# GpSimd computes the quantization factors, and the attention scores are made with the context stationary in two column tiles

## The chip, the core and the metric

The kernel runs on one core of a Trainium2 chip. The number told is the device time in microseconds of one execution, the median of several. A core has TensorE (matmul), VectorE, ScalarE and GpSimd, and SyncE issues the DMAs; each engine takes its own instructions in order, and they wait for each other through semaphores. In the profile these are PE (its weight loads PEld), DVE, ACT, POOL and SP.

## The reference

x is 8 batches of 512 tokens of 512 numbers, ctx_2048 is 8 contexts of 64 rows of 512, of which some are masked. An attention of the layer-normed tokens over the 64 context rows is added to x, and then a feed-forward part with ternary weights and inputs quantized per token; D is 512 and the hidden width H is 2048. Cut to what matters (LN and xattn stand for the written-out functions):

```python
def _linear_bit(x, w, g):
    xq = _act_quant(_rmsnorm(x, g))        # round(x * 127/max|x|) per row
    wq = _ternary_quant(w)                 # -1, 0, 1 times arctanh(mean|w|)
    return jnp.einsum('bsd,od->bso', xq, wq)

x = x + xattn(_layernorm(x), ctx_2048, mask)     # softmax(x ctx^T / sqrt(D)) ctx
h = silu(_linear_bit(LN(x), w1, g1)) * _linear_bit(LN(x), w2, g2)
x = x + _linear_bit(h, w3, g3)
```

_rmsnorm is g * x / sqrt(mean(x*x) + 1e-8), and _act_quant clips the row's maximum from below at 1e-4.

## The kernel before

The tokens are taken in 32 tiles of 128, four to a batch; X holds all of them in SBUF. The matmuls of the feed-forward part run in float16 on integers: the quantized inputs are numbers up to 127 times 2^-24, whose rounding is the quantization, and W1q, W2q, W3q hold the ternary weights. The work on a tile t is this:

- The a-stage makes the two quantized inputs of the up projections. GpSimd makes anm, the negated mean (stage_a_mean); ScalarE squares the centred tile (stage_a_var); VectorE multiplies the centred tile by the two gains into ga (stage_a_gain) and reduces it to the two maxima am (stage_a_max); GpSimd makes ak, the reciprocal root, with a power (stage_a_root). Then the factors (stage_a_factor, on VectorE): aa is am times ak with the floor, ar its reciprocal, af is ar times ak times 127. GpSimd multiplies ga by af into c12 (quantize_12), makes asc and asq from aa (stage_a_worth), and SyncE transposes c12 by DMA into q12T.
- up(t, n) for n = 0 to 3, on TensorE: 4 matmuls with W1q into the PSUM bank S1[n % 2] and 4 with W2q into S2[n % 2]. ScalarE makes silu from S1 (line 693), VectorE multiplies it by S2 into hp (gate, line 907), GpSimd multiplies by the gain g3 into gh (gain_3, line 521), VectorE takes the maximum of gh (max_3, line 913), and ScalarE squares hp in two halves (line 700).
- The h-stage makes the factor of the third quantization: GpSimd adds the two sums of squares into hs and makes hve and hk, a reciprocal root (stage_h_root); VectorE reduces the four maxima to hm1 (stage_h_top) and makes hkk, ha, the reciprocal hr and hf (stage_h_factor). ScalarE scales gh by hf into c3 (quantize_3, line 685), SyncE transposes c3 into q3T.
- down(t) on TensorE: 16 matmuls into DN (line 1191). VectorE makes hsc, the worth of the result (worth_3), and adds DN times hsc to x (result, line 947).

There is one ga, one c12, one am, ar, af and ak. So stage_a_gain of tile t + 2 waits until quantize_12 of tile t + 1 is done, and stage_a_gain waits for anm of its own tile.

The order is written out by hand: a batch is four slots j = 0 to 3, and slot j is one call of slot(b, j) in the program of each engine. In slot t = 4b + j TensorE runs up(t, 0), down(t - 2), up(t, 1), up(t, 2), up(t, 3). Batch 0, batches 6 and 7 are written out, and batches 1 to 5 are one hardware loop. The a-stage runs one to two tiles ahead of the up projections.

The attention of batch b + 1 runs within batch b: in slot 0 TensorE turns the centred context (attention_ccT) and makes the scores, VectorE the softmax's differences; in slot 1 ScalarE makes the exponentials, TensorE turns them and makes half of the readout, VectorE adds it to x (attention_x1, line 865); the other half follows in slots 2 and 3. attention_scores runs 16 float32 matmuls of 64 columns: the stationary operand is a block of 128 tokens of x, turned beforehand in HBM (xTs), and the moving one is ccT; the result lies with tokens on partitions in R[1], where VectorE reads it. attention on GpSimd makes the scale of the exponent (xve, xrs, rs) in slot 0.

## Time and profile before

| | |
|---|---|
| median of 3 runs | 471.03 us (470.67 to 472.04) |
| profiled execution | 472.33 us |
| its span, first to last instruction | 470.5 us |
| mean granted TensorE clock, share of full speed | 0.942 |
| TensorE busy | 409.9 us (87%) |
| VectorE busy | 407.1 us (87%) |
| ScalarE busy | 339.5 us (72%) |
| GpSimd busy | 341.3 us (73%) |

Busy time is the union of an engine's instructions, without its waits. The shares are means over a prologue (weights are loaded, summed and made ternary), the steady batches, and a last batch without attention; what one stage is bound by is read from that stage's rows. In a row of the timeline the first number is the start, the second how long the instruction or the merged group lasted, and the bracket at the end the idle time before it and what ended it. Neighbouring instructions overlap by some 0.03 to 0.17 us, so costs in a row of work are best taken from start to start.

### The profile page before, as it was taken

What the parts mean: (1) busy time and instruction counts of PE and PEld (TensorE: products, weight loads), DVE (VectorE), ACT (ScalarE), POOL (GpSimd) and SP (SyncE); (2) the same over time, 40 slices, a digit from 0 to 9 for tenths busy, and PEclk for the clock granted to TensorE, in tenths of its full rate; (3) what the DMA queues carried; (4) which work ended last, traced back from release to release, by engine and by line L of the source; (5) the groups of instructions that cost most, each with busy time, mean ns of one, the idle gap of its engine ahead of it and who ended that gap; (6) DMA issues with size and microseconds to landing.
All of it is one profiled execution on the core that took longest, in us unless ns stands there. A gap on an engine that the chain in (4) does not pass through costs nothing. (4 is left out here: it accounts for less than half of the span.)

```text
span 470.5 us, 8445 instructions
## 1 busy us (share of the span) xinstructions
PE 409.9 (87%) x1966; PEld 197.5 (42%) x1966; DVE 407.1 (87%) x927; ACT 339.5 (72%) x607; POOL 341.3 (73%) x539
## 2 busy tenths in 40 slices
PE   8326644899999999999999999999999999999995
PEld 8102412344644464446434543445444634334432
DVE  3799576889899999999999999999999999999662
ACT  1585446986798769886988788878886796666552
POOL 0267858787777787788788787778777877878650
PEclk9756795899999999999999999999999999999998
DMA  7999901545557455745574466447654444444431
GB/s 270 396 366 421 312 16 22 135 90 114 139 148 173 90 114 143 179 88 115 165 178 89 111 182 163 90 111 189 139 129 111 91 88 91 86 94 91 90 69 45
DMA packets 110504, 67.45 MB, mean 143 GB/s; under 512 B 100752, under 2 KB 100880, under 8 KB 106768
## 3 DMA queue, kind: packets, MB, share of 16 engines
q1 hardware_dynamic: 110480, 67.19, 53.9%
q8 instruction: 8, 0.13, 0.1%
q14 instruction: 16, 0.13, 0.1%
HBM read 34.14 MB, written 8.39 MB: 90 GB/s over the span
## 5 line engine op out<-in xcount | busy, mean ns | idle before, releaser
L521 POOL TENSOR_TENSOR stageB<-stageB,g3b 128x512 f32<-128x512 f32 x128 | 163.8, 1285 | 46.2 <-DVE stageB L907 45.3
L1163 PE MATMUL S<-W2q,q12T 128*128 128x512 f16 x512 | 134.5, 386 | 8.9 <-DVE stageB L907 6.2
L1163 PE MATMUL S<-W1q,q12T 128*128 128x512 f16 x512 | 135.3, 388 | 0.0
L693 ACT ACTIVATE sg<-S,asc 128x512 f32<-128x512 f32 x128 | 87.5, 683 | 54.1 <-PE S L1163 49.3
L1191 PE MATMUL DN<-W3q,stageB 128*128 128x512 f16 x512 | 118.7, 386 | 7.3 <-DMA stageB<-stageB 7.3
L907 DVE TENSOR_TENSOR stageB<-sg,S 128x512 f32<-128x512 f32 x128 | 86.7, 677 | 19.9 <-ACT sg L693 10.5
L913 DVE TENSOR_REDUCE hm<-stageB 128x1 f32<-128x512 f32 x128 | 86.5, 677 | 0.2 <-POOL stageB L521 0.2
L1163 PEld LDWEIGHTS S<-W2q,q12T 128*128 128x128 f16 x512 | 49.5, 99 | 75.3 <-DVE stageB L907 13.9
L1191 PEld LDWEIGHTS DN<-W3q,stageB 128*128 128x128 f16 x512 | 49.8, 99 | 70.3 <-issue 10.8
L1163 PEld LDWEIGHTS S<-W1q,q12T 128*128 128x128 f16 x512 | 49.8, 100 | 66.3 <-issue 10.1
L685 ACT ACTIVATE stageB<-stageB,hf 128x1024 f16<-128x1024 f32 x64 | 69.8, 1140 | 4.8 <-DVE hf L933 4.8
L700 ACT ACTIVATE junk<-stageB 128x1024 bf16<-128x1024 f32 x64 | 67.3, 1051 | 6.5 <-DVE stageB L907 5.9
L874 DVE SCALAR_TENSOR_TENSOR ga<-X,anm,g12b 128x512 f32<-128x512 f32 x64 | 56.8, 925 | 5.5 <-POOL c L510 3.8
L675 ACT ACTIVATE junk_a<-X,anm 128x512 bf16 (+1 forms) x32 | 23.0, 718 | 33.2 <-POOL anm L464 33.2
L510 POOL TENSOR_SCALAR c<-ga,af 128x512 f16<-128x512 f32 x64 | 43.5, 692 | 1.1 <-DVE af L898 1.0
L880 DVE TENSOR_REDUCE am<-ga 128x2 f32<-128x1024 f32 x32 | 38.7, 1209 | 0.0
L947 DVE SCALAR_TENSOR_TENSOR X<-DN,hsc,X 128x512 f32 (+1 forms) x32 | 24.0, 750 | 10.0 <-PE DN L1191 4.5
L1123 PEld LDWEIGHTS R<-ccT,xTs 128*128 128x128 f32 x256 | 30.0, 193 | 1.8 <-ACT ccT L632 0.6
L1123 PE MATMUL R<-ccT,xTs 128*128 128x64 f32 x256 | 29.6, 274 | 0.5 <-ACT ccT L632 0.5
L475 POOL TENSOR_TENSOR ak<-avk,mhalf 128x1 f32<-128x1 f32 x32 | 27.3, 853 | 2.7
L1151 PE MATMUL DN<-wabs,ones 128*128 128x5 f32 (+1 forms) x6 | 1.8, 365 | 26.6 <-DVE wabs L953 18.2
L865 DVE SCALAR_TENSOR_TENSOR X<-R,rval,X 128x512 f32 (+1 forms) x32 | 22.6, 744 | 1.8 <-PE R L1142 1.8
(112 smaller groups left out, 430.7 us busy)
## 6 DMA issues: line engine op xcount, KB each, us to landing
xTs<-in_xT SPq DMA_DIRECT2D x8, 1024.0 KB, 7.0
X<-in_x SPq DMA_DIRECT2D x8, 1024.0 KB, 6.0
out_x<-X SPq DMA_DIRECT2D x32, 256.0 KB, 2.9
X<-in_w1T SPq DMA_DIRECT2D x4, 1024.0 KB, 12.5
stageB<-in_w2T SPq DMA_DIRECT2D x4, 1024.0 KB, 20.4
X<-in_w3T SPq DMA_DIRECT2D x4, 1024.0 KB, 9.2
ctxr<-in_ctx SPq DMA_DIRECT2D x16, 128.0 KB, 3.1
ctxc<-in_ctx SPq DMA_DIRECT2D x8, 128.0 KB, 3.9
```

Of the source, the lines that this page charges most:

```text
L510: nc.gpsimd.tensor_scalar(c12[:, i * D:(i + 1) * D], ga[:, i, :], af[:, i:i + 1], QUANTUM, ALU.mult, ALU.mult).then_inc(s_c12_made, 1)
L521: nc.gpsimd.tensor_tensor(gh[q][:, part], hp[:, part], g3b[:, part], ALU.mult).then_inc(s_gh_made, 1)
L685: nc.scalar.activation(c3[:, part], gh[q][:, part], ACT.Copy, scale=hf[:, :]).then_inc(s_c3_made, 1)
L693: nc.scalar.activation(sg[n % 2][:, :], S1[n % 2][:, :], ACT.Silu, scale=asc[z][:, 0:1])\
L700: nc.scalar.activation(junk[:, h * HALF:(h + 1) * HALF], hp[:, h * HALF:(h + 1) * HALF], ACT.Square, accum_out=hss[:, h:h + 1]).then_inc(s ...
L874: nc.vector.scalar_tensor_tensor(out=ga[:, i, :], in0=xtile(t), scalar=anm[:, :], in1=g12b[:, i, :], op0=ALU.add, op1=ALU.mult).then_inc(s ...
L880: nc.vector.tensor_reduce(am[:, :], ga[:, :, :], AX_X, ALU.max, apply_absolute_value=True)\
L907: nc.vector.tensor_tensor(hp[:, n * CH:(n + 1) * CH], sg[n % 2][:, :], S2[n % 2][:, :], ALU.mult)\
L913: nc.vector.tensor_reduce(hm[:, n:n + 1], gh[q][:, n * CH:(n + 1) * CH], AX_X, ALU.max, apply_absolute_value=True).then_inc(s_gh_max, 1)
L1123: mm = nc.tensor.matmul(R[1][:, j * M:(j + 1) * M], xTs[:, k, j, :], ccT[:, k, :], start=(k == 0), stop=(k == KD - 1))
L1163: mm = nc.tensor.matmul(bank[n % 2][:, :], q12T[q][:, i * KD + k, :], w[:, n, k, :], start=(k == 0), stop=(k == KD - 1))
L1191: mm = nc.tensor.matmul(DN[:, :], q3T[:, k, :], W3q[:, k, :], start=(k == 0), stop=(k == KH - 1))
```

## The change

It has two parts.

**Factors.** stage_a_factor, stage_h_factor and worth_3 move from VectorE to GpSimd. VectorE keeps the reciprocals, and takes them of the maxima am and hm1 themselves, right behind the reductions. The factor is then made in one instruction as a minimum: af = min(ar * 1e-4, ak), and the constant 127 * 2^-24 / 1e-4 goes into quantize_12; hkk takes the same constant, ha = max(hm1 * hkk, 127 * 2^-24), hf = min(hr * 127 * 2^-24, hkk), and hsc takes the constant out again. aa and af are made for both columns at once, in one instruction each instead of two. hsc is now double, ha single.

**Scores.** The context ccT is the stationary operand, 64 columns wide, in two column tiles (columns 0 to 63 and 64 to 127 of the array): e = 0 takes the token blocks 0 and 2, e = 1 the blocks 1 and 3, 256 moving columns each; 8 matmuls instead of 16. The result has context rows on partitions. ScalarE copies it to half (attention_half), and two transposes on TensorE (attention_turn) bring it to the layout of before in R[1]. In the loop attention_half stands behind silu 1 of slot 0, ahead of the x squares and quantize_3, and attention_turn between up(t, 2) and up(t, 3).

The diff, cut to its core:

```diff
+            def stage_a_factor(t, z):
+                pool.wait_ge(s_a_am, t + 1)
+                pool.wait_ge(s_a_k, t + 1)
...
+                nc.gpsimd.tensor_scalar(aa[z][:, :], am[:, :], ak[:, :], ACT_MAX_FLOOR, ALU.mult, ALU.max)
...
+                pool.wait_ge(s_a_r, t + 1)
+                nc.gpsimd.tensor_scalar(af[:, :], ar[:, :], ACT_MAX_FLOOR, ak[:, :], ALU.mult, ALU.min)
...
@@ quantize_12
-                    nc.gpsimd.tensor_scalar(c12[:, i * D:(i + 1) * D], ga[:, i, :], af[:, i:i + 1], QUANTUM,
+                    nc.gpsimd.tensor_scalar(c12[:, i * D:(i + 1) * D], ga[:, i, :], af[:, i:i + 1], QMAX * QUANTUM / ACT_MAX_FLOOR,
...
@@ stage_h_root, behind hk
+                pool.wait_ge(s_h_k, t + 1)
+                nc.gpsimd.tensor_scalar(hkk[:, :], hk[:, :], asc[z][:, 1:2], QMAX * QUANTUM / ACT_MAX_FLOOR, ALU.mult, ALU.mult)
+            def stage_h_factor(t):
+                pool.wait_ge(s_h_kk, t + 1)
+                pool.wait_ge(s_h_max, t + 1)
...
+                nc.gpsimd.tensor_scalar(ha[:, :], hm1[:, :], hkk[:, :], QMAX * QUANTUM, ALU.mult, ALU.max)
+                pool.wait_ge(s_h_r, t + 1)
...
+                nc.gpsimd.tensor_scalar(hf[:, :], hr[:, :], QMAX * QUANTUM, hkk[:, :], ALU.mult, ALU.min)
+            def worth_3(t, q):
...
+                nc.gpsimd.tensor_scalar(hsc[q][:, :], ha[:, :], wc[:, 2:3], ACT_MAX_FLOOR / (QMAX * QUANTUM), ALU.mult, ALU.mult)
@@ slot of GpSimd
                     stage_h_root(t - 1, (j - 1) % NZ)
+                    stage_h_factor(t - 1)
+                    if not (first and j == 1):
+                        worth_3(t - 1, (j - 1) % 2)
                 if ahead:
                     stage_a_mean(t + 2, (j + 2) % TPB)
                 if not (last and j == TPB - 1):
+                    stage_a_factor(t + 1, (j + 1) % NZ)
                     quantize_12(t + 1)
@@ slot of ScalarE
                 if attn and j == 0 and not first:
+                    attention_half(b + 1)
                     two(x_square, b + 1, 2)
@@ VectorE: stage_a_max and stage_h_top get the reciprocal, stage_a_factor, stage_h_factor and worth_3 go
+                nc.vector.reciprocal(ar[:, :], am[:, :]).then_inc(s_a_r, 1)
...
+                nc.vector.reciprocal(hr[:, :], hm1[:, :]).then_inc(s_h_r, 1)
@@ TensorE
-                for j in range(TPB):
-                    for k in range(KD):
-                        mm = nc.tensor.matmul(R[1][:, j * M:(j + 1) * M], xTs[:, k, j, :], ccT[:, k, :],
-                                              start=(k == 0), stop=(k == KD - 1))
+                for k in range(KD):
+                    for e in range(2):
+                        mm = nc.tensor.matmul(R[1][e * M:(e + 1) * M, 0:TPB // 2 * P], ccT[:, k, :], xTs[:, k, e::2, :],
+                                              start=(k == 0), stop=(k == KD - 1), tile_position=(0, e * M))
+            def attention_turn(a):
+                pe.wait_ge(s_half_made, a + 1)
+                for i in range(TPB // 2):
+                    mm = nc.tensor.transpose(R[1][:, i * P:(i + 1) * P], half[:, i * P:(i + 1) * P], identf[:, :])
```

The first place is slot 3 of batch 0 on GpSimd, a slot without attention work there, from hs of tile t - 1 (behind gain_3) to the next gain_3. Of the kernel before:

```order
L526 TENSOR_TENSOR hs<-hss 128x1
L529 TENSOR_SCALAR hve<-hs,asq 128x1
L531 TENSOR_TENSOR hk<-hve,mhalf 128x1
L464 TENSOR_SCALAR anm<-x1sum 128x1
L510 TENSOR_SCALAR c<-ga,af 128x512 x2
L482 TENSOR_TENSOR asc<-aa,wc 128x2
L485 TENSOR_SCALAR asq<-asc 128x1
L521 TENSOR_TENSOR stageB<-stageB,g3b 128x512
```

and of the changed one:

```order
L544 TENSOR_TENSOR hs<-hss 128x1
L547 TENSOR_SCALAR hve<-hs,asq 128x1
L549 TENSOR_TENSOR hk<-hve,mhalf 128x1
L552 TENSOR_SCALAR hkk<-hk,asc 128x1
L561 TENSOR_SCALAR ha<-hm,hkk 128x1
L566 TENSOR_SCALAR hf<-hr,hkk 128x1
L574 TENSOR_SCALAR hsc<-ha,wc 128x1
L467 TENSOR_SCALAR anm<-x1sum 128x1
L487 TENSOR_SCALAR aa<-am,ak 128x2
L493 TENSOR_SCALAR af<-ar,ak 128x2
L528 TENSOR_SCALAR c<-ga,af 128x512 x2
L500 TENSOR_TENSOR asc<-aa,wc 128x2
```

Six instructions are new: four between hk and anm, two between anm and the quantization c.

The second place is the same slot on VectorE, from the last reduction of hm (tile t - 1) over ga (tile t + 2) to am. Of the kernel before:

```order
L919 TENSOR_REDUCE hm<-hm 128x1
L924 TENSOR_SCALAR hkk<-hk,asc 128x1
L927 TENSOR_SCALAR ha<-hm,hkk 128x1
L929 RECIPROCAL hr<-ha 128x1
L933 TENSOR_SCALAR hf<-hr,hkk 128x1
L874 SCALAR_TENSOR_TENSOR ga<-X,anm,g12b 128x512 x2
L907 TENSOR_TENSOR stageB<-sg,S_1 128x512
L940 TENSOR_SCALAR hsc<-ha,wc 128x1
L947 SCALAR_TENSOR_TENSOR X<-DN,hsc,X 128x512
L907 TENSOR_TENSOR stageB<-sg,S_0 128x512
L880 TENSOR_REDUCE am<-ga 128x2
```

and of the changed one:

```order
L969 TENSOR_REDUCE hm<-hm 128x1
L973 RECIPROCAL hr<-hm 128x1
L934 SCALAR_TENSOR_TENSOR ga<-X,anm,g12b 128x512 x2
L955 TENSOR_TENSOR stageB<-sg,S_1 128x512
L980 SCALAR_TENSOR_TENSOR X<-DN,hsc,X 128x512
L955 TENSOR_TENSOR stageB<-sg,S_0 128x512
L942 TENSOR_REDUCE am<-ga 128x2
L947 RECIPROCAL ar<-am 128x2
```

hkk, ha, hf and hsc are gone, hr is the reciprocal of hm, and ar now stands right behind am.

The third place is slot 0 of the loop on ScalarE, from silu 1 to silu 2. Of the kernel before:

```order
L693 ACTIVATE sg<-S_1,asc 128x512
L663 ISA
L663 ACTIVATE junk_x,xss<-X,xnm 128x512
L663 ISA
L663 ACTIVATE junk_x,xss<-X,xnm 128x512
L680 REGISTER_ALU
L685 ACTIVATE stageB<-stageB,hf 128x1024 x2
L692 REGISTER_ALU
L693 ACTIVATE sg<-S_0,asc 128x512
```

and of the changed one:

```order
L750 ACTIVATE sg<-S_1,asc 128x512
L689 COPY half<-R 128x256
L720 ISA
L720 ACTIVATE junk_x,xss<-X,xnm 128x512
L720 ISA
L720 ACTIVATE junk_x,xss<-X,xnm 128x512
L737 REGISTER_ALU
L742 ACTIVATE stageB<-stageB,hf 128x1024 x2
L749 REGISTER_ALU
L750 ACTIVATE sg<-S_0,asc 128x512
```

The copy into half stands between silu 1 and the two x squares; quantize_3 and silu 2 are behind it as before.

## Rows read from the trace of the kernel before

**Rows 1.** Busy us of PE, PEld, DVE, ACT, POOL in one loop batch; clock; DMA.

```profile
212.31:261.76 49.45, 48.35 (x240) 23.09 (x239) 46.69 (x110) 40.09 (x77) 39.26 (x61) 1.00 0.57 135
```

**Rows 2.** Waits in that batch: engine, line, waited-for: us in total, times, longest.

```profile
POOL stageB L521 <- DVE stageB L907: 6.4, 9, 1.6
...
PE S L1163 <- DVE stageB L907: 1.1, 2, 0.6
POOL hs L526 <- ACT junk L700: 1.1, 2, 0.6
```

**Rows 3.** Timeline of GpSimd in slots 0 and 1 of that batch.

```profile
222.92 0.19 POOL L449 TENSOR_SCALAR xve<-xss 128x4 f32<-128x4 f32 x1
...
224.73 2.50 POOL L521 TENSOR_TENSOR stageB<-stageB,g3b 128x512 f32<-128x512 f32 x2
227.72 0.19 POOL L526 TENSOR_TENSOR hs<-hss 128x1 f32<-128x1 f32 x1 [0.49 <-ACT junk L700]
...
228.44 0.55 POOL L531 TENSOR_TENSOR hk<-hve,mhalf 128x1 f32<-128x1 f32 x1
229.07 0.19 POOL L464 TENSOR_SCALAR anm<-x1sum 128x1 f32<-128x1 f32 x1
229.24 1.36 POOL L510 TENSOR_SCALAR c<-ga,af 128x512 f16<-128x512 f32 x2
...
230.93 0.27 POOL L485 TENSOR_SCALAR asq<-asc 128x1 f32<-128x1 f32 x1 [0.17 <-POOL asc L482]
...
233.10 0.94 POOL L475 TENSOR_TENSOR ak<-avk,mhalf 128x1 f32<-128x1 f32 x1
...
240.27 0.19 POOL L526 TENSOR_TENSOR hs<-hss 128x1 f32<-128x1 f32 x1 [0.58 <-ACT junk L700]
```

**Rows 4.** Timeline of VectorE: batch 0 slot 2, then slot 1 of the batch.

```profile
94.75 1.42 DVE L874 SCALAR_TENSOR_TENSOR ga<-X,anm,g12b 128x512 f32<-128x512 f32 x2 [0.30 <-POOL c L510]
...
230.75 0.16 DVE L919 TENSOR_REDUCE hm<-hm 128x1 f32<-128x4 f32 x1
...
231.79 1.84 DVE L874 SCALAR_TENSOR_TENSOR ga<-X,anm,g12b 128x512 f32<-128x512 f32 x2
233.55 0.20 DVE L940 TENSOR_SCALAR hsc<-ha,wc 128x1 f32<-128x1 f32 x1
233.97 0.75 DVE L947 SCALAR_TENSOR_TENSOR X<-DN,hsc,X 128x512 f32 x1 [0.21 <-DVE hsc L940]
...
237.55 0.68 DVE L907 TENSOR_TENSOR stageB<-sg,S 128x512 f32<-128x512 f32 x1
```

**Rows 5.** Instructions by line: duration ns min/median/max, first and last start us.

```profile
L529 POOL TENSOR_SCALAR hve<-hs,asq x32: 264/264/497, 70.3 to 456.9; 128x1 f32<-128x1 f32 x32
...
L1123 PE MATMUL R<-ccT,xTs x256: 218/275/324, 9.7 to 369.6; 128*128 128x64 f32 x128
...
L1142 PE MATMUL R<-ctxr,probT x64: 588/693/1220, 17.8 to 393.4; 64*128 64x512 f32 x64
```

**Rows 6.** Timeline of TensorE: batch 0, the loop batch, batch 7.

```profile
88.66 5.31 PE L1191 MATMUL DN<-W3q,stageB 128*128 128x512 f16 x16 [2.09 <-DMA stageB<-stageB]
...
217.89 3.68 PE L1123 MATMUL R<-ccT,xTs 128*128 128x64 f32 x32
...
231.77 0.38 PE L1130 MATMUL R<-identf,prob 128*128 128x128 f32 x2
...
236.33 1.13 PE L1142 MATMUL R<-ctxr,probT 64*128 64x512 f32 x4
...
410.79 3.61 PE L1191 MATMUL DN<-W3q,stageB 128*128 128x512 f16 x16 [1.14 <-DMA stageB<-stageB]
...
422.41 3.61 PE L1191 MATMUL DN<-W3q,stageB 128*128 128x512 f16 x16 [1.10 <-DMA stageB<-stageB]
```

**Rows 7.** Timeline of ScalarE in slot 0 of the loop batch.

```profile
219.42 2.18 ACT L685 ACTIVATE stageB<-stageB,hf 128x1024 f16<-128x1024 f32 x2
222.47 0.69 ACT L693 ACTIVATE sg<-S,asc 128x512 f32<-128x512 f32 x1 [0.87 <-PE S L1163]
```

More of the change, by code:

```diff
@@ L107, in bit_ffn_xattn @@
         identf = sb("identf", [P, P])
+        half = sb("half", [P, TPB // 2 * P])
         warm = sb("warm", [P, 4])
@@ L153, in bit_ffn_xattn @@
         hkk = sb("hkk", [P, 1])
-        ha = [sb(f"ha{i}", [P, 1]) for i in range(2)]
+        ha = sb("ha", [P, 1])
         hr = sb("hr", [P, 1])
         hf = sb("hf", [P, 1])
-        hsc = sb("hsc", [P, 1])
+        hsc = [sb(f"hsc{i}", [P, 1]) for i in range(2)]
         S1 = [ps(f"S1_{i}", [P, CH]) for i in range(2)]
@@ L630, in attention_ccT, with attention_half @@
                 if later(a):
+                    act.wait_ge(s_half_ps, a)
+                nc.scalar.copy(ccT[:, :, :].rearrange("p k m -> p (k m)"), CT[:, :]).then_inc(s_ccT_made, 1)
+            def attention_half(a):
+                act.wait_ge(s_half_ps, a + 1)
+                if later(a):
                     act.wait_ge(s_scores_ps, a)
-                nc.scalar.copy(ccT[:, :, :].rearrange("p k m -> p (k m)"), CT[:, :]).then_inc(s_ccT_made, 1)
+                nc.scalar.copy(half[:, :], R[1][:, 0:TPB // 2 * P]).then_inc(s_half_made, 1)
             def attention_exp(a):
@@ L879, in stage_a_max @@
                 dve.wait_ge(s_a_ga, 2 * (t + 1))
+                if later(t):
+                    dve.wait_ge(s_a_max, t)
                 nc.vector.tensor_reduce(am[:, :], ga[:, :, :], AX_X, ALU.max, apply_absolute_value=True)\
                     .then_inc(s_a_am, 1)
[L883 removed]
                 dve.wait_ge(s_a_am, t + 1)
[L886 to L899 removed]
+                if later(t):
+                    dve.wait_ge(s_a_f, t)
+                nc.vector.reciprocal(ar[:, :], am[:, :]).then_inc(s_a_r, 1)
             def gate(t, n):
@@ L946, in result @@
                 xt = xtile(t)
-                nc.vector.scalar_tensor_tensor(out=xt, in0=DN[:, :], scalar=hsc[:, :], in1=xt, op0=ALU.mult,
+                nc.vector.scalar_tensor_tensor(out=xt, in0=DN[:, :], scalar=hsc[q][:, :], in1=xt, op0=ALU.mult,
                                                op1=ALU.add).then_inc(s_x2_made, 1)
@@ L1041, in slot @@
                 if not early and j == 1:
-                    worth_3(t - 2, j % 2)
-                    result(t - 2)
+                    result(t - 2, j % 2)
                 gate(t, 1)
@@ L1053, in slot @@
                 if not early and j != 1:
-                    worth_3(t - 2, j % 2)
-                    result(t - 2)
+                    result(t - 2, j % 2)
                 if attn and j < 3:
                     stage_a_max(t + 2)
-                if first and j == 1:
-                    stage_h_factor(0, 0, 0)
                 gate(t, 2)
@@ L1198, in _ @@
             attention_scores(0)
+            attention_turn(0)
             attention_probT(0)
@@ L1228, in slot @@
                     attention_scores(a)
+                if attn and j == 0 and not first:
+                    attention_turn(a)
                 up(t, 3, q)
+                if first and j == 0:
+                    attention_turn(a)
                 if attn and j == 1:
```

92 lines of the change are left out of this document (44 added, 48 removed).

## The prediction, made before the changed kernel ran

> **What bounds the kernel now.** I read one steady batch before the shares of the page. In the 49.45 us of a loop batch TensorE works 48.35 us and VectorE 46.69, GpSimd only 39.26 [rows 1]. The waits of the same batch say who has room: GpSimd waits 6.4 us for the gate products of VectorE and 1.1 us for the squares of ScalarE, TensorE 1.1 us for gate products [rows 2]. So these two set the batch together, and GpSimd has 7.5 us of air: its instructions with their own gaps need 49.45 - 7.5 = 42.0 us. Shares are not enough here, because the change puts work on a chain that crosses GpSimd, VectorE and ScalarE. I followed that chain through one slot of the timeline on each of them [rows 3, 4, 7].
>
> **VectorE part of the change.** Each slot loses seven small steps there (aa twice, af twice, hkk, ha, hf, and hsc behind them) and keeps its two reciprocals, which now read the maxima directly. Between the last reduction of hm at 230.75 and ga at 231.79 the four h steps fill 1.04 us [rows 4]; with the reciprocal alone I take 0.3. hsc and the wait behind it take 233.55 to 233.97, 0.42 [rows 4]. The a-factors, five steps like these, take about 0.8. Less 0.2 for the reciprocal behind am, VectorE is relieved of some 1.8 us a slot, 7 us a batch.
>
> **GpSimd part.** It gains hkk, ha, hf, hsc, aa and af, six instructions a slot of a form that it runs now as hve (a scalar taken from a tile): 0.264 us [rows 5]. One that needs the one before waits 0.17 us more, as asq does [rows 3]. Step by step: hk to hkk 0.72 where hk to anm is 0.63 now; hkk to ha 0.44; ha, hf and hsc 0.25 each: +1.3 us between hs and anm. aa 0.25, and af 0.27 + 0.17 before the quantization may start: +0.7. Together **+2.0 us a slot**, 8.0 a batch. Added to 42.0 that makes 50.0 us a batch even if GpSimd never waited, 0.55 more than the batch takes now. Bounds for one such instruction are 0.19 us (anm) [rows 3] and 0.50 (the longest hve) [rows 5], so 1.5 to 3.4 us a slot.
>
> **Where these 2.0 us stand.** They stand ahead of quantize_12, and VectorE's ga, one tile further on, waits for quantize_12 (there is one ga and one c12). Behind ga stand gate 1, result, am, gate 2 and gate 3 in VectorE's order, and behind gate 3 the next hs. Now the quantization ends at 229.24 + 1.36 = 230.60 [rows 3] and ga starts at 231.79 [rows 4]: 1.2 us of slack. VectorE will be ready for ga 0.7 us sooner and GpSimd 2.0 later, so the slack becomes a wait of 1.5. The trace has this wait once, at 94.75, where ga waits for c [rows 4]. Hence I close the loop and add it up:
> hs to the end of quantize_12: 227.72 to 230.60, 2.9 now [rows 3], 4.9 then, and 0.1 to the start of ga.
> ga to gate 3: 231.79 to 237.55, 5.8 now [rows 4]; less 0.42 (hsc); less 0.4, because the ga pair next to a GpSimd that has just ended its quantization takes 1.42 (at 94.75) and not 1.84 [rows 4]; plus 0.2 for the reciprocal: 5.15.
> gate 3 to hs: 237.55 to 240.27 is 2.7 [rows 3, 4], with hs held up 0.58 by a square that stands behind a late silu; without that it would be 2.1. I take 2.4.
> Sum: **12.55 us a slot**. A batch now takes 49.45 / 4 = 12.36 a slot with all the attention work in it; this is without it.
>
> **The attention work on top.** ha also needs the last maximum of hm, which VectorE reaches behind gate 3, two maxima, gate 0 of the next tile and a third maximum: four steps of 0.6 and 0.9 for the last two reductions, 3.3 us after gate 3. GpSimd asks for it 2.4 + 1.9 = 4.3 after. What VectorE has besides comes in between: rval and the x1 pair, 1.8 us (slot 1), the centring of ctx, 1.55 (slot 2), the x1 pair, 1.35 (slot 3). These are estimates from five steps of 0.2 to 0.75 each. GpSimd stalls 0.8 and 0.6, and 0.6 behind slot 3, where gate 2 stands ahead of am and hs comes 0.3 sooner. In slot 0 GpSimd itself is the longest: 4.9 + 3.5 (to the end of ak at 234.04) + 1.25 + 1.8 (222.92 to 224.73) + 2.5 [rows 3] + 0.2 = 14.15, with 0.6 of stall 14.75. Slots 1, 2 and 3: 12.55; 13.35; 12.55 - 0.3 + 0.6 = 12.85. The batch is 53.5 us, **+4.05**.
> For the five loop batches and batch 6: 24.3. Batch 0: its slots 1 to 3 carry the 2.0 us each, less 1.4 for the shorter score block of slot 0 and 1.1 of VectorE's relief in slots that wait for weights: +3.5. Batch 7: two slots prepare a tile ahead and go from 11.6 us (410.79 to 422.41) [rows 6] to 12.25: +1.2. Its last two still wait for the q3 transposes; in the tail hkk, ha and hf pass to GpSimd: +0.2. Sum: 24.3 + 3.5 + 1.2 + 0.2 = **+29.2 us**.
>
> **TensorE part.** The scores are 32 records in 3.68 us [rows 6]. Now there are 8 matmuls of 256 columns, 16 records. By the least durations, 218 ns for 64 columns and 588 for 512 [rows 5], a column of a record costs 0.83 ns and a record 0.21 us: all sixteen 3.4 us one behind the other, 1.7 if the two column tiles run at once. No row has column tiles. The nearest has row tiles: the readout streams four records of 0.42 us, 1.7 in all, and takes 1.13 [rows 6], so they overlap and lose a third of the gain. I take 2.1 us, and 0.4 for the two transposes, as those of prob at 231.77 [rows 6]. TensorE gains 1.2 us a batch, between a loss of 0.1 and a gain of 1.6. In the forecast this is worth nothing, since TensorE then idles 2 us a slot; it counts if TensorE still sets the batch.
> The page "TensorE: Matmul & The Clock Gate" of the Trainium skill (Part 3, Packing small matmuls) says that matmuls in different column groups run together, a few ns apart. By that the block is 1.7 us, and my sum stays what it is; no run here shows it yet.
> ScalarE's copy of half waits for the score block, with the x squares, quantize_3 and silu 2 behind it. Now quantize_3 starts at 219.42 and silu 2 at 222.47, after 0.87 of wait for TensorE [rows 7]. The block would end near 217.9 + 2.1 = 220.0, the copy 220.5, two squares 221.9, quantize_3 224.0, silu 2 then: 1.5 later. In slot 0 GpSimd's attention steps are longer than that and cover it; without that cover it costs 1.5 us a batch. The same copy ahead of the first weight sum on ScalarE in the prologue I give nothing, and 0 to 1 us in the range.
>
> **Rivals.** (B) GpSimd only adds up and the loop does not bind: 0.55 x 6 = 3.3 us, and about 2 for batches 0 and 7: 476. For it: VectorE has won 1.8 us a slot and could catch up. Against it: ga's wait is written into the order of both engines.
> (C) Faster: the six instructions fall into GpSimd's 7.5 us of waits, and TensorE, relieved of 1.2 us a batch, sets the time: with a little of its wait for gates 1.35 x 7 = 9.5 less, 461.5. It decides from where a moved instruction costs under 0.15 us with its wait, or ga doesn't wait for c12. Against it: none under 0.19 [rows 3].
> (D) Slower still: behind a wait of 2.09 us at 88.66 the next 16 matmuls took 5.31 us, elsewhere 3.61 [rows 6]. If the new pauses bring that, or the 1.5 us of half are not covered, or a moved instruction takes 0.35: 506 to 520, say 512.
> (E) Gain and loss cancel: within 0.3% of 471.0.
>
> **How the numbers follow.** The profiled execution took 472.33 us with a span of 470.5, 1.3 over the median of 471.03. Span 470.5 + 29.2 = 499.7, that execution 501.5, the median 500.2, which is the forecast; its own range is 486 to 508. Chances: forecast 0.62, B 0.15, C 0.10, D 0.10, E 0.03. The range of 479 to 514 leaves out C, E and a part of B and D. Faster by over 0.3% (about what a measurement of this kernel can tell from no change) 0.10, within 0.3% 0.04, slower 0.86.
>
> **What would show it.** Right: ga waits for c on GpSimd in nearly every slot, 1 to 2 us; GpSimd busy above 85%, VectorE below 80%; a loop batch of 52 to 55 us; ha waits for hm behind an x1 pair; small GpSimd groups of 0.26 us. Wrong: TensorE busy 98% of a batch still, or a batch near 48. Whether the column tiles run at once is read off the score block: near 2 us, or near 3.4.

## The result, and the profile after

| | before | changed |
|---|---|---|
| median | 471.53 us (470.67 to 472.22, 4 runs) | 531.9 us (531.25 to 532.18, 4 runs) |
| ratio, with its 95% interval | | 1.1275 (1.124 to 1.131) |
| span of the profiled execution | 470.5 us | 530.2 us |
| VectorE busy | 407.1 us (87%) | 357.8 us (67%) |
| GpSimd busy | 341.3 us (73%) | 401.9 us (76%) |
| mean granted TensorE clock | 0.942 | 0.926 |

The change costs 60 us where 29 were forecast, and the time lies outside the range (479 to 514). The direction and the place are as forecast. First a steady batch, from the start of anm to that of anm four slots later; the columns are those of [rows 1], the last but two is the granted clock as a share of full speed:

```profile
core 0: us, PE busy (x) PEld busy (x) DVE busy (x) ACT busy (x) POOL busy (x), PEclk, DMA share, GB/s
240.71:298.92 58.21, 50.32 (x227) 20.32 (x226) 40.86 (x76) 40.12 (x77) 47.06 (x84) 0.97 0.48 115
```

The batch took 49.45 us before [rows 1] and takes 58.2 now; 53.5 was forecast. The waits for other engines in the same stretch on GpSimd, and two waits of the whole execution (engine, waiting instruction, releaser, us in total, times, longest):

```profile
POOL ha L561 <- DVE hm L969: 1.9, 2, 1.0
POOL hs L544 <- ACT junk L757: 1.7, 1, 1.7
POOL stageB L539 <- DVE stageB L955: 0.5, 2, 0.2
...
DVE ga L934 <- POOL c L528: 118.9, 29, 5.7
PE S L1188 <- DVE stageB L955: 34.5, 28, 2.6
```

VectorE waits for quantize_12 in 29 slots, 4 us each time; before it did so twice, 3.8 us in all, and in no loop batch. What a batch is without GpSimd's waits for other engines I call GpSimd's own length (its instructions, their gaps, and its waits for itself): 58.2 - 1.9 - 1.7 - 0.5 = 54.1 us. The same stretch of the kernel before, from anm to anm (216.33 to 265.77), has 1.1 us of waits at hs and this one, so its own length is 49.45 - 7.0 = 42.4 us (the prediction's batch starts elsewhere and has 7.5 us of waits):

```profile
POOL stageB L521 <- DVE stageB L907: 5.9, 8, 1.6
```

So the own length alone is now longer than the whole batch was, and longer than the forecast for it (50.0). This is the stretch of slot 2 on GpSimd:

```profile
267.86 0.19 POOL L544 TENSOR_TENSOR hs<-hss 128x1 f32<-128x1 f32 x1 [1.67 <-ACT junk L757]
268.22 0.27 POOL L547 TENSOR_SCALAR hve<-hs,asq 128x1 f32<-128x1 f32 x1 [0.17 <-POOL hs L544]
268.57 0.55 POOL L549 TENSOR_TENSOR hk<-hve,mhalf 128x1 f32<-128x1 f32 x1
269.29 0.26 POOL L552 TENSOR_SCALAR hkk<-hk,asc 128x1 f32<-128x1 f32 x1 [0.17 <-POOL hk L549]
269.75 0.31 POOL L561 TENSOR_SCALAR ha<-hm,hkk 128x1 f32<-128x1 f32 x1 [0.19 <-POOL hkk L552]
270.05 0.30 POOL L566 TENSOR_SCALAR hf<-hr,hkk 128x1 f32<-128x1 f32 x1
270.45 0.27 POOL L574 TENSOR_SCALAR hsc<-ha,wc 128x1 f32<-128x1 f32 x1
270.80 0.19 POOL L467 TENSOR_SCALAR anm<-x1sum 128x1 f32<-128x1 f32 x1
271.08 0.32 POOL L487 TENSOR_SCALAR aa<-am,ak 128x2 f32<-128x2 f32 x1
271.50 0.33 POOL L493 TENSOR_SCALAR af<-ar,ak 128x2 f32<-128x2 f32 x1
272.07 1.47 POOL L528 TENSOR_SCALAR c<-ga,af 128x512 f16<-128x512 f32 x2 [0.25 <-POOL af L493]
273.62 0.20 POOL L500 TENSOR_TENSOR asc<-aa,wc 128x2 f32<-128x2 f32 x1
273.99 0.65 POOL L503 TENSOR_SCALAR asq<-asc 128x1 f32<-128x1 f32 x1 [0.17 <-POOL asc L500]
274.61 1.71 POOL L539 TENSOR_TENSOR stageB<-stageB,g3b 128x512 f32<-128x512 f32 x1
```

and where asc starts in [rows 3], in the kernel before:

```profile
230.56 0.20 POOL L482 TENSOR_TENSOR asc<-aa,wc 128x2 f32<-128x2 f32 x1
```

From start to start: hs to anm 2.94 us (1.35 in [rows 3]), anm to c 1.27 (0.17), c to asc 1.55 (1.32). That is 2.9 us more a slot; the sum of the prediction had 2.0. Each moved instruction lasts 0.26 to 0.33 us, and where nothing waits the next one mostly starts 0.08 to 0.10 us behind its end, not at it (hf, which follows ha at once, is the exception).

TensorE's side, the score block and what follows it in slot 0, and two matmul groups of slot 1; the last row is ScalarE's, the silu that reads the next group of TensorE:

```profile
240.76 1.95 PE L1142 MATMUL R<-xTs,ccT 128*64 128x256 f32 x16
242.64 1.04 PE L1188 MATMUL S<-W1q,q12T 128*128 128x512 f16 x4
...
261.48 1.89 PE L1188 MATMUL S<-W2q,q12T 128*128 128x512 f16 x4 [1.46 <-DVE stageB L955]
263.30 1.75 PE L1167 MATMUL R<-ctxr,probT 64*128 64x512 f32 x4
...
266.06 0.69 ACT L750 ACTIVATE sg<-S,asc 128x512 f32<-128x512 f32 x1 [2.59 <-PE S L1188]
```

The score block takes 1.88 us from start to start where it took 3.52 (3.68 is its duration in [rows 6]): the two column tiles ran at the same time, since the prediction's own figures gave 3.4 us for one behind the other and 1.7 for both at once. The readout in slot 1 took 1.75 us instead of 1.13 [rows 6]. And the stretch around these two:

```profile
258.00:267.00 9.00, 6.55 (x22) 2.21 (x23) 7.99 (x14) 6.40 (x11) 7.53 (x9) 0.81 0.69 141
```

The granted clock is 0.81 here, so a part of this stretch ran at 1.2 and not at 2.4 GHz; just before its two long rows TensorE had waited 2.21 us for silu 1 and 1.46 us for gate 1. What the clock can cost is seen in other batches: of the changed kernel, its fourth loop batch and batch 6, and batch 6 of the kernel before:

```profile
298.92:358.32 59.40, 51.84 (x220) 20.59 (x220) 40.93 (x76) 40.11 (x77) 47.03 (x85) 0.91 0.46 113
416.58:472.66 56.08, 49.30 (x229) 20.60 (x228) 38.77 (x73) 36.12 (x64) 46.43 (x84) 1.00 0.35 76
...
364.56:412.85 48.29, 46.40 (x229) 22.25 (x228) 46.22 (x109) 35.98 (x63) 39.09 (x60) 1.00 0.41 88
```

At 0.91 the batch is 1.1 us longer than the four at 0.97 (58.2 to 58.4). And where the clock never fell, in batch 6, the change still costs 7.8 us of the 8.8 of a loop batch. So the clock is a small part of the loss.

### The profile page after: what moved, and what is told of

Its sections match the earlier page's. It is cut to its first block, busy times and chain, and to the rows that moved or that the text cites. A ratio compares the mean times of both kernels' runs of the same rounds, so it can differ in the third digit from the quotient of the medians.

```text
span 530.2 us, 8453 instructions
## 1 busy us (share of the span) xinstructions
PE 416.9 (79%) x1854; PEld 174.1 (33%) x1854; DVE 357.8 (67%) x671; ACT 340.4 (64%) x615; POOL 401.9 (76%) x731
## 4 chain that ended last, share of the span: by engine, by line
POOL 35%; issue 23%; DVE 19%; PE 10%; DMA 5%; ACT 3%; POOLq 2%; SPq 1%; DVEq 1%; ACTq 0%
POOL stageB L539 14%; PE S L1188 6%; DVE hm L961 5%; DVE stageB L955 5%; POOL c L528 4%; DMA X<-in_w1T 3%; DMA q12T<-c 2%; POOL af L493 2%; POOL hk L549 2%; PE DN L1216 2%; DVE ga L934 2%; POOL aa L487 2%; PE R L1167 2%; DVE am L942 2%; DVE X L925 1%
## 5 line engine op out<-in xcount | busy, mean ns | idle before, releaser
L539 POOL TENSOR_TENSOR stageB<-stageB,g3b 128x512 f32<-128x512 f32 x128 | 175.3, 1381 | 5.1 <-DVE stageB L955 4.3
L1188 PE MATMUL S<-W2q,q12T 128*128 128x512 f16 x512 | 140.4, 399 | 37.3 <-DVE stageB L955 34.5
L1188 PE MATMUL S<-W1q,q12T 128*128 128x512 f16 x512 | 138.5, 395 | 22.1 <-ACT sg L750 15.7
L934 DVE SCALAR_TENSOR_TENSOR ga<-X,anm,g12b 128x512 f32<-128x512 f32 x64 | 45.4, 751 | 118.9 <-POOL c L528 118.9
L1216 PE MATMUL DN<-W3q,stageB 128*128 128x512 f16 x512 | 116.1, 379 | 4.6 <-DMA stageB<-stageB 3.0
L750 ACT ACTIVATE sg<-S,asc 128x512 f32<-128x512 f32 x128 | 84.8, 679 | 44.1 <-PE S L1188 28.6
L1188 PEld LDWEIGHTS S<-W1q,q12T 128*128 128x128 f16 x512 | 46.9, 101 | 102.3 <-ACT sg L750 34.1
L528 POOL TENSOR_SCALAR c<-ga,af 128x512 f16<-128x512 f32 x64 | 44.6, 696 | 10.5 <-POOL af L493 7.7
L561 POOL TENSOR_SCALAR ha<-hm,hkk 128x1 f32<-128x1 f32 x32 | 10.0, 313 | 18.4 <-DVE hm L969 15.4
L1167 PE MATMUL R<-ctxr,probT 64*128 64x512 f32 x64 | 23.3, 812 | 0.5 <-ACT probT L702 0.5
L503 POOL TENSOR_SCALAR asq<-asc 128x1 f32<-128x1 f32 x30 | 17.9, 597 | 5.1 <-POOL asc L500 5.1
```

What stands on the lines that cost most here:

```text
L528: nc.gpsimd.tensor_scalar(c12[:, i * D:(i + 1) * D], ga[:, i, :], af[:, i:i + 1], QMAX * QUANTUM / ACT_MAX_FLOOR, ALU.mult, ALU.mult).then ...
L539: nc.gpsimd.tensor_tensor(gh[q][:, part], hp[:, part], g3b[:, part], ALU.mult).then_inc(s_gh_made, 1)
L750: nc.scalar.activation(sg[n % 2][:, :], S1[n % 2][:, :], ACT.Silu, scale=asc[z][:, 0:1])\
L934: nc.vector.scalar_tensor_tensor(out=ga[:, i, :], in0=xtile(t), scalar=anm[:, :], in1=g12b[:, i, :], op0=ALU.add, op1=ALU.mult).then_inc(s ...
L1167: mm = nc.tensor.matmul(R[e][:, :], probT[e * M:(e + 1) * M, i, :], ctxr[e * M:(e + 1) * M, :], start=True, stop=True)
L1188: mm = nc.tensor.matmul(bank[n % 2][:, :], q12T[q][:, i * KD + k, :], w[:, n, k, :], start=(k == 0), stop=(k == KD - 1))
```

## The experiments

A kernel is called below by the first part of its name, as m1. In all of them the DMAs that transpose c12 and c3 are plain copies of the same 256 KB, so that the transposition is left out (the edit of c12 is shown). With this edit alone the changed kernel is l1 and the kernel before is q1, the control:

```diff
-                sp.dma_start_transpose(q12T[q][:, :, :], c12[:, :]).then_inc(s_q12_in, 16)
+                sp.dma_start(q12T[q][:, :, :].rearrange("p k q -> p (k q)"), c12[:, :]).then_inc(s_q12_in, 16)
```

> A control. The changed kernel with the transposing DMAs of c12 and c3 written as plain DMA copies of the same 256 KB from the same tile to the same tile, behind the same waits: what it leaves out is the transposition itself, so the matmuls multiply numbers in another order. The transposing DMAs took 3.1 us from issue to landing, the store of a tile of 256 KB 2.9 us. The loss lies on GpSimd, VectorE and the gates, not on the transposing DMAs: 528 to 535 us, a ratio to the kernel before of 1.12 to 1.14. If the transposing DMAs were part of the loss (TensorE waits for q12T 13 times in the changed kernel), it would come out under 520 us. Every kernel of the study has this replacement.

Measured 531.5 us, 1.126 of before (1.122 to 1.130), as expected: nothing of the loss lies in those DMAs.

> A control. The kernel before with the transposing DMAs of c12 and c3 written as plain DMA copies (the transposition is left out), nothing else. In the trace of the kernel before TensorE waits for no transposed tile in a loop batch, so the 0.8 us by which the copies land sooner should be worth nothing but in the last batch: 469 to 472 us. If the copies gave something in each batch, it would be 463 to 468 us, and the gains of the kernels with the new scores would be that much smaller.

Measured 469.06 us, 0.995 (0.993 to 0.998). The copies land in 2.3 us, and give the kernel before 2.2 us in all, as expected; a batch of it is 49.47 us, so none of it in a loop batch. The ratios below are all to the kernel before itself, so 0.995 is what "no change" is in them, and 469.1 us.

**The two parts of the change apart.** First the scores alone, and the factors alone.

> The kernel before with the new scores alone (column tiles, the copy to half, two transposes); the factors stay on VectorE. The transposing DMAs are plain copies (the transposition is left out). If TensorE sets the time of slot 0 in the kernel before, the score block (3.68 us before, 1.88 + 0.4 us in the changed kernel) gives back up to 1.4 us in each of 7 batches: 8 to 10 us below the kernel before. If the loop over quantize_12, ga, the gates and the sum of squares sets slot 0, or the copy to half comes late on ScalarE, nothing is won: within 2 us of it. In neither case can the scores be part of the 60 us lost; a time 10 us above it would say that they are.

Measured 470.8 us, 1.000 (0.996 to 1.003): TensorE's gain is lost, as in the second case. The times of m1 and the control (469.1) are hardly apart for their spread, but the loop batches are: 50.0 us against 49.5. ScalarE shows why, slot 0 of a loop batch:

```profile
217.10 0.19 POOL L467 TENSOR_SCALAR anm<-x1sum 128x1 f32<-128x1 f32 x1
...
220.75 0.37 ACT L641 COPY half<-R 128x256 f32<-128x256 f32 x1 [1.87 <-PE R L1135]
...
222.44 2.17 ACT L694 ACTIVATE stageB<-stageB,hf 128x1024 f16<-128x1024 f32 x2
...
224.52 1.24 ACT L702 ACTIVATE sg<-S,asc 128x512 f32<-128x512 f32 x2
```

The copy to half waits 1.87 us for the score block and holds up quantize_3 and silu 2 behind it. Silu 2 starts 7.4 us behind anm, where it was 222.47 - 216.33 = 6.1 [rows 3, 7]: 1.3 us late, nearly all of the 1.4 that TensorE had won (3.52 - 1.88 - 0.22).

> The changed kernel with the old scores (16 matmuls of 64 columns, read by VectorE as they stand); the factors are on GpSimd. The transposing DMAs are plain copies (the transposition is left out). Theory (the chains over GpSimd make the whole loss, and TensorE waits for them): within 3 us of the changed kernel, 528 to 535 us, since the longer score block falls into TensorE's waits. Rival (the new scores, whose copy holds ScalarE up, or whose pause lets TensorE's clock fall, are a part of the loss): 510 to 525 us.

Measured 532.2 us, 1.131 (1.124 to 1.138). As the theory said, the whole loss is that of the factors; with the factors on GpSimd the scores count for nothing, either way.

**The factors apart.** h-factors (hkk, ha, hf, hsc) alone, and a-factors (aa, af) alone on GpSimd.

```diff
@@ m2, slot of GpSimd
-                    stage_a_factor(t + 1, (j + 1) % NZ)
...
@@ m2, slot of VectorE, behind max_3(t, 1)
+                if ahead:
+                    stage_a_factor(t + 2, (j + 2) % NZ)
```

> The changed kernel with aa and af back on VectorE (by the old rule); hkk, ha, hf and hsc stay on GpSimd. The transposing DMAs are plain copies (the transposition is left out). On GpSimd the four took 2.0 us from the start of hkk to the start of anm less the 0.1 us that anm had to wait for before; aa and af took 0.8 us. Theory (a loop with a slack): hs to the end of c is 5.7 - 0.8 = 4.9 us, the loop 4.9 + 0.2 + 5.3 + 2.4 = 12.8 us where TensorE alone wants 12 us, that is 0.8 us a slot in 29 slots under the changed kernel, 24 us: 505 to 511 us. Rival (the loss is not in proportion to the length of the chain but comes from pauses of TensorE and its clock once there are any): 520 us or more.

Measured 510.4 us, 1.083 (1.076 to 1.091), in the theory's interval, but not for the reason it gave. A batch of 55.2 us:

```profile
POOL ha L546 <- DVE hm L964: 5.7, 4, 1.7
...
POOL hs L529 <- ACT junk L740: 0.4, 1, 0.4
```

GpSimd's own length is 49.1 us there, no more than a batch takes before. It stalls 1.6 to 1.7 us in three of four slots at ha, which wants the last maximum from VectorE, and quantize_12 stands behind that stall. The same kernel gives another reading of the clock: two of its loop batches ran at 1.00 and took 55.2 us, one at 0.97 took 55.2 as well, and the first two, at 0.97, took 55.7 and 55.4.

```diff
@@ p4, slot of GpSimd
-                    stage_h_factor(t - 1)
-                    if not (first and j == 1):
-                        worth_3(t - 1, (j - 1) % 2)
...
@@ p4, slot of VectorE, behind stage_h_top
+                    if not early:
+                        stage_h_factor(t - 1, (j - 1) % NZ, (j - 1) % 2)
...
+                    worth_3(t - 2, j % 2)
```

> The changed kernel with hkk, ha, hf and hsc back on VectorE; aa and af stay on GpSimd, directly ahead of quantize_12. The transposing DMAs are plain copies (the transposition is left out). aa and af with their gaps took 1.1 us a slot and the quantization 0.2 longer, so GpSimd's own length is 42.4 + 5.2 = 47.6 us a batch, and hs to the end of c 4.2 us; the loop is 4.2 + 0.2 + 5.6 + 2.4 = 12.4 us, as long as a slot is now (12.4). Theory (nothing is paid until a chain passes the slot's own length): 470 to 480 us. Rival (each chain crosses GpSimd and VectorE in every slot, so that its length is paid at once): 1.3 us x 30 = 39 us more, 510 us.

Measured 473.4 us, 1.003 (1.001 to 1.006), 4 us over the control, as the theory said. But p4 has the new scores too, so its equal without the moved factors is m1. Here is a batch of m1, and below it one of p4:

```profile
230.16:280.19 50.03, 47.38 (x226) 20.52 (x224) 46.65 (x110) 40.13 (x78) 39.43 (x61) 1.00 0.38 133
...
242.20:292.25 50.05, 47.65 (x226) 20.37 (x224) 44.08 (x93) 40.13 (x77) 42.38 (x69) 1.00 0.39 135
```

The own length rose from 42.4 to 48.1 us (50.05 us of batch, 2.0 of waits), and the batch by nothing against m1: 5.7 us more work on GpSimd, all of it in its former waits. Against m1 (470.8 us) the h-factors alone cost 40 us, the a-factors alone 3, both together (l1) 61.

**Where the chain is closed.** Three kernels take one link each out of the changed kernel.

```diff
-                    stage_h_root(t - 1, (j - 1) % NZ)
-                    stage_h_factor(t - 1)
-                    if not (first and j == 1):
-                        worth_3(t - 1, (j - 1) % 2)
                 if ahead:
                     stage_a_mean(t + 2, (j + 2) % TPB)
...
                     stage_a_factor(t + 1, (j + 1) % NZ)
                     quantize_12(t + 1)
+                if not (first and j == 0):
+                    stage_h_root(t - 1, (j - 1) % NZ)
+                    stage_h_factor(t - 1)
+                    if not (first and j == 1):
+                        worth_3(t - 1, (j - 1) % 2)
```

> The changed kernel with another order on GpSimd: anm, aa, af and c12 come ahead of hs, hve, hk, hkk, ha, hf and hsc instead of behind them. Every instruction is there, on the same engine. The transposing DMAs are plain copies (the transposition is left out). Theory (the place in front of quantize_12 is what costs, since ga and the gates wait for it): from gate 3 to the end of c it is gain_3 1.3 us + anm, aa, af, c 2.6 us = 3.9 us instead of 2.4 + 5.7 = 8.1 us, the loop is about 9.4 us and no longer sets the slot; TensorE (12 us a slot) and GpSimd's own sum (47 us busy and some 5 us of its own waits a batch, 52 us against 49.5 us) do: 475 to 490 us. Rival (the sum of the work on GpSimd or the slower clock makes the loss, whatever the order): 515 us or more.

Measured 506.0 us, 1.072 (1.064 to 1.080), between the theory and the rival. The batch is 54.35 us:

```profile
227.34:281.69 54.35, 49.25 (x226) 20.92 (x224) 40.80 (x77) 40.09 (x77) 46.45 (x86) 0.97 0.35 123
```

```profile
POOL anm L467 <- DVE X L927: 0.4, 1, 0.4
```

This 0.4 us is all that GpSimd waits for another engine. So 3.9 us a batch belonged to the order (25.6 us in all), and what is left is GpSimd's own length, 53.95 us, with nothing between.

```diff
-        ga = sb("ga", [P, 2, D])
+        gas = [sb(f"ga{i}", [P, 2, D]) for i in range(2)]
...
-                if later(t):
-                    dve.wait_ge(s_c12_made, 2 * t)
+                if later(t, 2):
+                    dve.wait_ge(s_c12_made, 2 * (t - 1))
```

> The changed kernel with two buffers for ga, so that ga of tile t + 2 waits for anm, but no longer for c12 of tile t + 1 (the copy half of the scores lies in the buffer sm to make room). The transposing DMAs are plain copies (the transposition is left out). Theory: VectorE goes on when anm is there, 3.1 us behind hs instead of 5.7 us, so the loop is 2.6 us shorter, 14.5 - 2.6 = 11.9 us a slot, about TensorE's 12 us: 470 to 490 us, unless the maximum of ga comes so much earlier that nothing else waits. Rival (the end of quantize_12 counts by another way, the DMA of c12 to TensorE or gain_3 0 behind it on GpSimd, which the gates of the next slot wait for): 510 us or more.

Measured 510.5 us, 1.081 (1.073 to 1.090), in the rival's range, but by neither way that was named. The wait of ga for c is gone, but ga waits for anm instead:

```profile
DVE ga L936 <- POOL anm L467: 44.1, 29, 3.2
```

anm too stands behind ha and hsc, and ScalarE's silu 1 behind the square that wants anm. The loop batches take 53.8 and 55.2 us in turn, of which 52 are GpSimd's own length and 1.5 to 3.1 its waits for others. The expectation counted the loop over c only, and missed both.

```diff
-                part = slice(n * CH, (n + 1) * CH)
+                part = slice(n * CH, n * CH + (CH // 4 if n == 1 else CH))
```

> The changed kernel with gain_3 of chunk 1 on 128 columns instead of 512 in every tile (three quarters of that product are left out; the transposing DMAs are plain copies, the transposition is left out). It takes 0.8 us a slot off GpSimd at a place outside the loop of the prediction (hs, quantize_12, ga, gate 3, hs). Theory now (GpSimd's own length is the bound, wherever an instruction stands): 0.8 x 31 = 25 us less than the changed kernel, of which its waits for others take a few back: 505 to 513 us. Rival (the loop of the prediction is the bound, GpSimd is full only because it waits inside the loop): 526 to 532 us.

Measured 528.9 us, 1.121 (1.115 to 1.126): the rival's range. My theory of that moment, that the length of GpSimd alone is the bound, fell. The batch still is 58.3 us:

```profile
POOL ha L561 <- DVE hm L969: 4.7, 4, 1.6
POOL stageB L539 <- DVE stageB L955: 3.0, 3, 1.1
```

The own length fell from 54.1 to 50.4 us, and the waits for others rose from 4.1 to 7.9. The second chain, which the shorter GpSimd lays bare, can be followed through slot 1:

```profile
254.06 0.31 POOL L561 TENSOR_SCALAR ha<-hm,hkk 128x1 f32<-128x1 f32 x1 [1.17 <-DVE hm L969]
...
258.06 1.42 DVE L934 SCALAR_TENSOR_TENSOR ga<-X,anm,g12b 128x512 f32<-128x512 f32 x2 [3.96 <-POOL c L528]
...
263.36 0.68 DVE L955 TENSOR_TENSOR stageB<-sg,S 128x512 f32<-128x512 f32 x1
...
268.69 0.16 DVE L969 TENSOR_REDUCE hm<-hm 128x1 f32<-128x4 f32 x1
...
269.01 0.31 POOL L561 TENSOR_SCALAR ha<-hm,hkk 128x1 f32<-128x1 f32 x1 [1.61 <-DVE hm L969]
```

The third row is gate 3, the fourth the last reduction of hm. From ha to ga it is 4.0 us (hf, hsc, anm, aa, af and c), from ga to gate 3 5.3, and from gate 3 to the next ha 5.65, with rval and the x1 pair in between: 14.95 us, which is the length of this slot. The loop goes over VectorE and back.

> The changed kernel with both cuts: quantize_12 with anm, aa and af ahead of the h-stage, and gain_3 of chunk 1 on 128 columns instead of 512 (three quarters of that product are left out; the transposing DMAs are plain copies, the transposition is left out). Theory (two chains side by side, GpSimd's own length and the loop over quantize_12, ga, gate 3 and ha): with the loop cut by the order, the 0.8 us a slot now count in full, since GpSimd had no wait left: own length 53.95 - 3.3 = 50.7 us a batch against 54.35, 3.3 to 3.6 us x 7.5 = 25 to 27 us less than the order alone (506 us): 479 to 483 us. Rival (TensorE with its slower clock, or something else not seen, holds the kernel with the new order): 2 to 5 us less as without the new order, 500 to 504 us.

Measured 483.3 us, 1.025 (1.020 to 1.030), just above the theory's interval. The same 0.8 us a slot that gave 2.6 us in the changed kernel give 22.7 us once the order has cut the loop; the batch is 51.5 us, of which GpSimd waits 0.6. So two chains stood side by side in the changed kernel. The loop through ha and quantize_12, at 58 us a batch, was the longer one: shortening only the other gave 2.6 us, cutting the loop gave 25.6 (m3), down to GpSimd's own length at 54, and from there the 0.8 us count in full.

**The price without VectorE.**

```diff
                     stage_h_root(t - 1, (j - 1) % NZ)
+                    extra(t - 1)
...
+                for i in range(6):
...
+                    nc.gpsimd.tensor_scalar(dum[:, i:i + 1], src, mhalf[:, 0:1], 1.0, ALU.mult, ALU.mult)
```

> The kernel before with six more instructions on GpSimd between hk and anm of each slot, a chain in the form of hkk (128 x 1, a scalar from a tile), each waiting for the one before, that nobody reads; nothing is taken from VectorE. The transposing DMAs are plain copies (the transposition is left out). Six of 0.27 + 0.19 us are 2.8 us a slot, 11.1 us a batch: GpSimd's own length becomes 42.4 + 11.1 = 53.5 us, the same as in the changed kernel less 0.9. Theory (length of GpSimd plus its waits for others, 0 to 4 us a batch): batch 54 to 58 us, 508 to 530 us. If VectorE, which here keeps its 46.7 us a batch, has to come into the loop with all its old steps, the waits grow: 535 us or more. If the moved instructions cost so much only because of what they wait for (am, hm), this one stays under 500 us.

Measured 515.5 us, 1.090 (1.084 to 1.096), in the theory's range: six instructions that want nothing of VectorE cost 46 us over the control, where the change costs 62. Two of the six in a row:

```profile
236.07 0.27 POOL L543 TENSOR_SCALAR dum<-dum,mhalf 128x1 f32<-128x1 f32 x1 [0.17 <-POOL dum L543]
236.50 0.26 POOL L543 TENSOR_SCALAR dum<-dum,mhalf 128x1 f32<-128x1 f32 x1 [0.17 <-POOL dum L543]
```

The batch is 54.8 us at a granted clock of 1.00 (the three at 0.97 took 55.6, 56.4 and 55.6), GpSimd's waits for others 1.4, so its own length 53.4, 0.1 off the expectation. VectorE had all its old work (45.5 us busy in that batch) and was no hindrance. The changed kernel takes 3.4 us a batch more, 0.7 of own length and 2.7 of waits for others, of which 1.9 at ha: what six instructions cost that need something from VectorE, beside six that don't (a part of the 3.4 can be the clock, 0.97 there).

**Looking for a version that gains.**

```diff
                 if attn and j == 0 and not first:
+                    two(x_square, b + 1, 2)
                     attention_half(b + 1)
-                    two(x_square, b + 1, 2)
```

> The kernel before with the new scores, and on ScalarE in slot 0 the pair of x squares ahead of the copy to half instead of behind it. The transposing DMAs are plain copies (the transposition is left out). With the copy first, ScalarE waited 1.87 us for the score block, quantize_3 began 5.3 us behind anm instead of 3.1, and silu 2 7.4 us behind anm instead of 6.1, 1.3 us late. Theory (this wait gives TensorE's gain back): the squares (1.4 us) fall into the wait, silu 2 comes 1.3 us earlier, and slot 0 of six or seven batches 1.0 to 1.3 us shorter: 461 to 465 us. Rival (VectorE, 46.7 us busy in a batch of 50, or the order of GpSimd in slot 0 hold the slot at 12.7 to 13.0 us anyway): 468 to 472 us.

Measured 467.9 us, 0.991 (0.988 to 0.995), just under the rival's range: 2.9 us less than the scores alone, and 1.2 less than the control, which is within the spread of the control's times (467.3 to 472.0). The copy now waits 0.46 us, not 1.87, and the batch is 49.4 instead of 50.0, against 49.47 in the control: slot 0 is 0.36 us shorter than there, slot 1 0.29 longer. TensorE is busy 47.2 us of the batch, so something else holds it; p1 below shows that VectorE does, at least for a part.

> The kernel of the run before, and the a-factor by the new rule, but on VectorE: the reciprocal of am directly, aa and af one instruction each for both columns instead of two. The h-factor stays as it was before. The transposing DMAs are plain copies (the transposition is left out). VectorE loses two small instructions a slot, some 0.3 us (aa twice 0.32, af twice 0.34 before; one of each two columns wide now). If VectorE is on the path in most slots, 0.3 us x 28 = 8 us less than the run before; if TensorE or the loop is, 0 to 2 us less. In the first case 454 to 458, in the second 460 to 465 us.

Measured 478.6 us, 1.016 (1.012 to 1.020): 11 us slower than n1, neither case. The one instruction for two columns takes three and a half times as long as one for one column:

```profile
L908 DVE TENSOR_SCALAR aa<-am,ak 128x2 f32<-128x2 f32 x32 | 23.0, 719 | 0.0
```

```profile
216.50 1.27 POOL L524 TENSOR_TENSOR stageB<-stageB,g3b 128x512 f32<-128x512 f32 x1 [1.07 <-DVE stageB L922]
216.84 0.15 DVE L898 RECIPROCAL ar<-am 128x2 f32<-128x2 f32 x1
216.91 0.90 DVE L908 TENSOR_SCALAR aa<-am,ak 128x2 f32<-128x2 f32 x1
...
231.24 0.20 DVE L908 TENSOR_SCALAR aa<-am,ak 128x2 f32<-128x2 f32 x1
```

The first row is the group of all 32 (busy us and mean ns). Below, aa starts beside a gain_3 of GpSimd and ends at 217.81, gain_3 at 217.77; in the last row no gain_3 runs, and it takes 0.20 us. In n1 the two narrow ones took 202 ns each.

```diff
                 gain_3(t, 0, j % 2)
+                if not (first and j <= 1):
+                    worth_3(t - 1, (j - 1) % 2)
```

> The kernel before with the new scores, the x squares ahead of the copy to half, and one of the moved instructions alone: hsc is made on GpSimd, behind the first gain_3 of the slot, so behind quantize_12 and outside the loop. The transposing DMAs are plain copies (the transposition is left out). GpSimd's own length goes from 42.4 to about 43.8 us a batch, VectorE loses hsc and the wait behind it, 0.42 us a slot, 1.7 of its 46.7 us a batch. Theory (a moved instruction costs nothing where GpSimd has room and nothing waits behind it, and VectorE is on the path): 0.2 to 0.4 us x 28 = 5 to 11 us under the same kernel without it (467.9 us): 457 to 463 us. Rival (TensorE and ScalarE hold the batch, VectorE's relief is not on the path): 465 to 469 us.

Measured 458.5 us, 0.973 (0.970 to 0.977), as the theory said. One moved instruction of six, behind quantize_12 and where its input is there, takes 9.3 us off n1; with the scores and the swap it is 10.5 us off the control. The batch is 48.14 us, TensorE busy 47.21 of it, VectorE 46.09. This kernel is faster than both kernels, by 2.2% with the copies on both sides; with the transposing DMAs it was not run.

## Why the prediction was wrong in size

- **What bounds the kernel now** (the one before is meant): right. TensorE and VectorE set it; GpSimd had 7.0 to 7.5 us of air (p4: 5.7 us a batch more on it, no longer a batch than m1).
- **The size of the moved instructions**: here the sum fails. "+2.0 us a slot" was six times the duration of hve and some waits; from start to start it is 2.9, since each one lasts 0.26 to 0.33 us, leaves a gap of 0.1 where it waits for nothing, and the quantization came to 1.55 us. In a batch that would be 3.6 of the 4.7 us that are missing, and in 29 slots 26 of the missing 31 us, if each slot paid it in full. Slot by slot the forecast is short by 0.3 us (slot 0), 2.5, 0.9 and 1.0: slots 2 and 3 miss by just this, slot 0 by less, slot 1 by more. The bounds of the prediction (1.5 to 3.4 a slot) held it; the value taken, by the nearest form, was too near to the low end. D's 0.35 us is near what a moved instruction takes from start to start where nothing waits (0.30 to 0.42), but D had too small a chance and too little time.
- **The loop hs, quantize_12, ga, gates, hs**: the mechanism is right (m3, n3: what counts is what stands ahead of quantize_12). hs to the end of c was 5.7 us, not 4.9; ga to gate 3 5.30, not 5.15; gate 3 to hs 2.27 in slot 2, 2.4 forecast. The wait of ga for c, from which the loop was argued, stands in the trace of before twice and not once: 3.52 us at 72.96 too.
- **The stall at ha for the last maximum**: named, but held for an addition in three slots. It is the second way through the same loop, and the longer one in every slot once GpSimd is shorter (n3).
- **Slot 1**: forecast 12.55, measured 15.0 us. 0.8 are the instructions, and 1.4 lie between gate 3 and hs (3.8 us, 2.4 forecast): hs waits 1.67 us for a square behind a silu that waited 2.59 for TensorE, which had come out of two waits and, for a part of the stretch, at the lower clock. How much of this slot is the clock and how much the waits no run tells apart. For the whole loss the rows above do: batch 6 at 1.00 lost 7.8 us as well.
- **Slot 0**: GpSimd is the longest there, as forecast (15.1 us, 14.75 forecast; the stall at ha of 0.6 did not come). The copy to half costs nothing in the changed kernel (p3; it waits 0.27 us in this batch), and with the old factors it makes silu 2 1.3 us late, forecast 1.5 (m1).
- **The score block**: 1.88 us, and 0.22 for the two transposes; 2.1 and 0.4 were taken. It was worth nothing, as said. By the page "TensorE: Matmul & The Clock Gate" of the Trainium skill (Part 3, Packing small matmuls) it would be 1.7, an estimate; the trace agrees that column groups run together.
- **Prologue, batch 0 and tail**: batch 0 grew by 7.75 us up to anm of its end, not 3.5; its slots 2 and 3 went from 11.3 and 11.8 to 13.8 and 13.7 us. Batch 6 grew by 7.8, batch 7 and the tail by 0. With 44.3 for the five loop batches the sum is 59.9, the spans differ by 59.7. So 28 of the 31 us that the forecast misses lie in the loop batches and batch 6.
- **The signs**: VectorE waits for c in 29 slots, as said, but 4 us and not 1 to 2 each time. VectorE is below 80% busy (67%), but GpSimd is not above 85%: it is 76%, and 81% of the batch, since the gaps and the waits for itself, which make its own length 93% of the batch, are not counted as busy.
- **Rivals**: B (GpSimd only adds up) had the right form for the kernel with the other order, at 54 us a batch instead of 50.0; C needs instructions under 0.15 us, or such that nothing waits behind: p1 is that case, with one instruction.

## What to carry to other kernels

Before small instructions move to an engine, add its own length from start to start, with gaps and with its waits for itself, and then follow the loop that crosses the engines; when two such chains are near each other (58 and 54 us here), shortening the shorter one gives next to nothing (2.6 us), cutting the longer one gives only the distance between them (25.6 us), and after that the first cut gives all (22.7 us). An instruction costs nothing on its new engine where it stands behind the one that others wait for and its input is already there: hsc, placed so, gained 9 us by VectorE's relief. In front of that one it costs nothing as long as there is slack (aa and af alone, p4), and its length once the slack is used up: all six cost 60 us. A gain on TensorE has to be followed to the next engine's queue: the copy that the new scores need took it back, and with that cured 1.2 us came out, no more than the spread, until VectorE was relieved too.
